# Gathers of v that wait for a free buffer of a ring of 40 instead of an earlier landing, with sixteen weighted rows and six banks for q

## What is computed

```python
for l in range(2):
    q = (x @ Wq[l] + bq[l]).reshape(N, H, D)       # k and v likewise
    a = (q[dst] * k[src]).sum(-1) * scale
    amax = segment_max(a, dst);  e = exp(a - amax[dst])
    denom = segment_sum(e, dst); alpha = e / (denom[dst] + 1e-16)
    agg = segment_sum(alpha[:, :, None] * v[src], dst)
    x = agg + (x @ Ws[l] + bs[l]) + enc
```

## Time and profile before

| what | us |
|---|---|
| median of three runs | 3386.14 (3384.03 to 3386.51) |
| the profiled execution, whole | 3403.18 |
| its span | 3401.4 |
| layer 0: first k gather issued, first v gather issued | 347.75, 774.83 |
| layer 0: last reduce of scores starts, first v product starts | 799.97, 841.80 |
| layer 0: last v gather issued, last v products start | 1265.48, 1269.47 |
| layer 1: first k gather issued, last v gather issued | 1532.71, 2455.14 |

### The profile page before, as it was taken

One profiled execution on the slowest core, in us unless ns is written; L12 is line 12 of the kernel. 1 busy time (PEld: TensorE's weight loads), 2 busy tenths in 40 slices (PEclk: granted clock), 3 DMA queues, 4 the chain that ended last, 5 costly groups with the idle time before them and its releaser, 6 DMA issues. The chain is left out here.

```text
span 3401.4 us, 43825 instructions
## 1 busy us (share of the span) xinstructions
PE 2660.2 (78%) x9872; PEld 1887.6 (55%) x9872; DVE 2266.3 (67%) x3504; ACT 829.6 (24%) x1638; POOL 1642.9 (48%) x1559
## 2 busy tenths in 40 slices
PE   2999787664877778997876658777776799969998
PEld 1788343333655556873443336555555577647776
DVE  5666688888766655446898887666547345476655
ACT  0454222221000011002222210000145323155544
POOL 0110667665566651106676656666514235344444
PEclk8999567776999998995667769999988899979999
DMA  1654666664566665436666646666642422261111
GB/s 58 211 197 171 196 195 198 193 191 124 161 194 198 198 184 180 139 115 200 193 199 194 193 116 173 192 194 193 183 168 99 136 99 99 85 198 38 37 37 36
DMA packets 215838, 524.38 MB, mean 154 GB/s; under 512 B 30652, under 2 KB 48424, under 8 KB 215238
## 3 DMA queue, kind: packets, MB, share of 16 engines
q0 software_dynamic: 100160, 328.28, 34.0%
q1 hardware_dynamic: 98182, 161.91, 14.2%
q10 hardware_dynamic: 17280, 31.63, 2.5%
HBM read 439.83 MB, written 81.88 MB: 153 GB/s over the span
## 5 line engine op out<-in xcount | busy, mean ns | idle before, releaser
L1488 PE MATMUL edge_psA<-layer_q_space 128*128 128x256 f32 (+1 forms) x2656 | 670.2, 400 | 200.0 <-DVE layer_q_space L1374 185.8
L1251 POOL DMA_INDIRECT edge_ring<-v_rows,edges_src x626 | 615.1, 983 | 370.6 <-DMA edge_ring<-v_rows,edges_src 197.3
L1251 POOL DMA_INDIRECT edge_ring<-k_rows,edges_src x626 | 591.5, 945 | 322.4 <-DMA edge_ring<-k_rows,edges_src 173.7
L1443 PE MATMUL edge_psQ<-layer_q_space,edge_hotT 128*128 x1328 | 575.3, 582 | 170.0 <-DVE layer_y_space L1296 132.6
L1488 PEld LDWEIGHTS edge_psA<-layer_q_space 128*128 128x128 f32 x2656 | 489.3, 193 | 380.7 <-issue 318.2
L1374 DVE TENSOR_TENSOR layer_q_space<-edge_ring,edge_psQ 128x512 f32<-128x512 f32 x664 | 434.6, 683 | 171.2 <-SPq L1219 168.0
L1443 PEld LDWEIGHTS edge_psQ<-layer_q_space,edge_hotT 128*128 128x128 f32 x1328 | 337.9, 279 | 373.2 <-issue 317.9
L1296 DVE TENSOR_TENSOR layer_y_space<-edge_psQ,edge_ring 128x512 f32<-128x512 f32 x664 | 423.7, 682 | 138.1 <-issue 52.1
L106 PE MATMUL proj_psP<-proj_w,proj_xT 128*128 128x512 f32 x1920 | 470.8, 403 | 12.6 <-DVE proj_w L886 5.5
L106 PEld LDWEIGHTS proj_psP<-proj_w,proj_xT 128*128 128x128 f32 x1920 | 361.8, 191 | 99.5 <-DVE proj_w L886 6.9
L1280 DVE TENSOR_REDUCE layer_scores<-layer_y_space 128x32 f32<-128x2048 f32 x166 | 377.6, 2275 | 0.1
(11 more groups left out here) (290 smaller groups left out, 2835.7 us busy)
## 6 DMA issues: line engine op xcount, KB each, us to landing
agg_rows<-layer_q_space ACTq DMA_DIRECT2D x40, 260.0 KB, 3.7
base_rows<-proj_enc SPq DMA_DIRECT2D x40, 256.0 KB, 2.0
k_rows<-proj_out ACTq DMA_DIRECT2D x40, 256.0 KB, 2.9
v_rows<-proj_out ACTq DMA_DIRECT2D x40, 256.0 KB, 2.5
edge_ring<-k_rows,edges_src POOLq DMA_INDIRECT x626, 3.7
edge_ring<-v_rows,edges_src POOLq DMA_INDIRECT x626, 3.7
ffn_downT<-down_rows SPq DMA_DIRECT2D x11, 512.0 KB, 10.2
proj_agg<-agg_rows SPq DMA_DIRECT2D x20, 260.0 KB, 3.0
```

The costliest lines, as they stand in the source:

```text
L1251: pool.indirect_dma_start(ring[:, (n + 1) % NB, :], None, rows, bass.IndirectOffsetOnAxis(ap=T["src"][:, t:t + 1], axis=0)).then_inc(lande ...
L1443: last = pe.matmul(psQ[i][:], hotT[j % 2][:, i * P:(i + 1) * P], one(qp[:, k, bass.ds(tiles[i], 1), :]), start=(k == 1), stop=(k == 0))
L1488: last = pe.matmul(psA[:, bass.ds(d % 2, 1), e, 0:hi - lo].rearrange("p o w -> p (o w)"), hot[:, s % R, :], wv[:, s % R, lo:hi], start=Fal ...
```

## The change

Five things change, all in `edge_attention` and the table that it reads.

1. The ring has NV = 40 buffers. k uses the first 32, and `prod` lies in the last eight during the k part. v uses all 40.
2. Gathers of k keep the wait for the landing three before. Gathers of v wait for no landing: the first 32 wait on `multiplied` as before, the next eight wait until all scores are reduced (`prod` is free), and gather t from 40 on waits until `weighted` has counted t - 40 + 21.
3. `wv` and `hot` have R = 16 rows instead of 8, so DVE starts a group at s when PE has summed slots up to s - 13.
4. q has six banks instead of four: two of `psA`, unused in the k part, are added.
5. PE waits for `hots` and `beside` once a group of 4 instead of in each slot. The arrival tables begin at other values (`K_FIRST`, `V_FIRST`) so that v starts at buffer 0.

```diff
-V_FIRST = ET % NB + 1
+NV = 40
+K_FIRST = NB - ET % NB
+V_FIRST = NV
...
-        B, R = 4, 8
+        B, R, QB = 4, 16, 6
...
-        ring = m.sb("ring", [P, NB, C])
+        ring = m.sb("ring", [P, NV, C])
...
-        prod = y_space[:, 0:2 * B * C].rearrange("p (i c) -> p i c", c=C)
-        cut = 2 * B * C
+        prod = ring[:, NB:NB + 2 * B, :]
+        cut = 0
...
+        psQ = [m.ps(f"psQ{i}", [P, C]) for i in range(B)] + [psA[:, 0, i, :] for i in range(QB - B)]
...
+        buffer = [(n + K_FIRST) % NB for n in range(ET)] + [t % NV for t in range(ET)]
+        landing = [(landed[u], 16 * buffer[:n + 1].count(u)) for n, u in enumerate(buffer)]
...
-                    if n >= FLIGHT:
-
-                        old = n - FLIGHT
-                        pool.wait_ge(landed[(old + 1) % NB],
-                                     old // NB * 16 + 16 if (old + 1) % NB else (old + 1) // NB * 16)
+                    if FLIGHT <= n < ET:
+
+                        pool.wait_ge(*landing[n - FLIGHT])
...
                     if t < NB:
                         pool.wait_ge(multiplied, min(n - NB + NT + 1, USED))
+                    elif t < NV:
+
+                        pool.wait_ge(reduced, BATCHES)
                     else:
-                        pool.wait_ge(weighted, t - NB + NT + 1)
+                        pool.wait_ge(weighted, t - NV + NT + 1)
...
-                        if j:
-
-                            pe.wait_ge(multiplied, j * B + i - B + 1)
+                        if j * B + i >= QB:
+
+                            pe.wait_ge(multiplied, j * B + i - QB + 1)
...
-                    pe.wait_ge(hots, s // B + 1)
-                    pe.wait_ge(beside, s // B + 1)
+                    if s % B == 0:
+                        pe.wait_ge(hots, s // B + 1)
+                        pe.wait_ge(beside, s // B + 1)
```

## The result

The changed kernel takes **3268.0 us** (median of 4 runs, 3264.0 to 3270.2) against 3385.1 us before (4 runs, 3381.2 to 3386.5), a ratio of 0.965 with a 95% interval of 0.964 to 0.967. It is faster by 117 us. The forecast was 3250 in a range of 3225 to 3292. The profiled execution takes 3264 us where that of before took 3403, so between the two traces there are 139 us.

A forecast was written before the change was run, and what follows sets the result against it. POOL's gathers, held by landing waits, were taken to bound the v part, and the k part was tied to POOL too. Layers gain 69.6 and 71.5 us, less 2 each: 137; 3386 - 137 = 3249, say 3250 us, range 3225 to 3292.

The forecast's parts named there:

- What bounds the v part: v part: runs at POOL's gather pace, 1.445 us each; 56 us a layer are waits beyond the floor, mostly under landings.
- The pace of 1.25 us: v part without the landing wait: POOL issues a gather every 1.25 us, its floor, and PE and DVE stay faster.
- Rival (a): v part: the DMA engines, or one, cap the pace above 1.25 us; at 1.35 the time is 3303; chance 0.13.
- (c): Slower: with only buffers limiting flight, landings lengthen and the stream slows; at 1.60 us a gather, 3440; chance 0.03.
- (d): v part: landings did not hold POOL, gaps stay; eight gathers and earlier start give 29 us, 3357; chance 0.02.
- Rival (b): k part: PE's banks made POOL's landings bunch, so k gains 10 us a layer instead of 2: 3233; chance 0.12.
- The eight more buffers and the start: v part: 273 gathers left instead of 281, at 1.25 us 64.6 and 66.5 us less; POOL resumes 3 us earlier.
- less 2 each: End of each layer: 2 us set against the gain, since a late landing there finds no slack in flight.
- The cover: Between the parts: the eight extra gathers cost nothing, done near 840, or 843 if blocked, long before they are needed.
- The banks of q: k part: six banks bounded per layer by 6 us won and 3 lost; 2 us won taken.
- The wait of DVE for PE in steady flow: v part: with sixteen rows the 25.4 us that L1364 waits for PE vanish, but buy nothing by themselves.
- The median: Last step: before's median lies 17 us below its profiled execution, carried over: 3386 - 137 = 3249, say 3250.

## Why the prediction was right, and where it was off

**What bounds the v part: right.** POOL's gathers, held by landings beyond 3.75 us. Taking out the landing wait alone (103 us) and keeping it alone (36 us of gain left) showed it from both sides, and a wait for the landing five before, which cost next to nothing, showed that it is the depth.

**The pace of 1.25 us: right to the digit.** 272 steps in 340.0 us in both layers. PE and DVE stayed below it. Rival (a), a cap by the DMA engines, is refuted up to this pace: their share rose to 0.76, forecast 0.77, and the stream to the 224 GB/s forecast. Rivals (c) and (d) are refuted as well: the median landing stayed at 3.7 us with no limit on the flight but the buffers, and the gaps went. Rival (b), 10 us a layer from the k part by the banks, is refuted too: with eight rows and four banks the way to the first v product was only 4.3 and 1.7 us longer.

**The eight more buffers and the start: right.** 64.6 + 3 and 66.5 + 3 us, less 2 each, were forecast for the v part. From DVE's first v product to the end of its last there were 429.0 and 431.1 us before and 362.3 and 362.4 after, so 66.7 and 68.7 less against 65.6 and 67.5. The pace made up some 54 a layer of it, the eight gathers and the earlier start the rest. The block that the Trainium skill names (SBUF — State Buffer, section Terms) showed under the second mask step, where the trace of before had no gather: a gather that began 1.1 us after the step took 2.75 us and ended 0.8 us after it. Under the six subtractions after it it did not show: the gathers there took 1.02 and 0.95. The cover held either way.

**The banks of q: right in size, hard to see.** I took 2 us a layer. From the first k gather to the first v product the change was -1.3 and -4.3 us in the first pair of traces, and +3.2 and -1.3 with the changed kernel's first later trace. Differences of 3 us between sessions hide a gain of 2. Within one session four banks and eight rows cost 4.3 and 1.7 us there, and 0.4 and 1.5 with free k gathers.

**The wait of DVE for PE in steady flow: read wrongly.** I expected the 25.4 us ahead of L1364 to vanish. After the change 18.6 us are still put down to PE there, and before and after it DVE's register instructions reach up to the end of nearly every such gap. Since the sum counts nothing for it, the forecast is not touched.

**The median: 18 us too low, and the step that failed is the last one.** The sum of 137 us against the profiled execution of before gave 3266; the profiled execution after took 3264. I then carried over the difference of 17 us between the profiled execution of before and its median. That difference is no property of a profiled execution: in three other sessions the kernel before runs at 3402 to 3405, profiled or not, and in two of them the changed one at 3275. The timed runs of before were faster by 17 us beside the result, those of the changed kernel by only 7. So of the 137, 127 came where both ran at their usual level, and 117 in the session of the result.

**The 2 us between 3266 and 3264 are partly luck.** Against the trace of before, the first trace of the changed kernel is 135.4 us shorter in the v parts and 5.6 from the first k gathers to the first v products, and 1.5 longer in all the rest. Its later trace on another chip is 134.3 shorter in the v parts, where 133 were forecast, but 1.9 longer in the k parts, where 4 less were forecast, and 3.5 longer in the rest, which the change doesn't touch. By these two traces that is 8 of the 10 us that the 127 lack to the 137. The changed kernel's profiled execution there is 10.5 us longer than the first one, mainly in the gathers of k (429.4 and 427.8 us in place of 425.0 and 424.3 from the first to the last), which still wait for landings.

Why before ran at 3385 in one session of four stays open. Landings shorter there would explain it, since they price both kernels and before the most, but the trace beside it took 3403 us, like those of the later sessions, so it can't show what made the timed runs faster.

**What I did not see: the k part.** I wrote that the landing wait stays there and priced everything else. I read it as tied to POOL, at 1.365 us a gather, and the same arithmetic would have given 313 x (1.365 - 1.25) = 36 us a layer. With the k gathers free, the way from the first of them to the first v product was 39.5 and 37.7 us shorter than in the changed kernel of the session.

## What to carry to other kernels

A wait for the landing of the n-th transfer before sets a pace: n issues must cover the late landings, not the median one. Here three in flight covered 3.75 us of a landing of 3.7 at the median and 6 at worst in the v part, and cost 0.19 us on each of 562 gathers; five cost next to nothing. Read the gaps of the issuing engine against its gap where nothing is waited for, and apply the finding to every stream of the kernel that has the same wait. And a forecast that rests on one profiled execution should give the change as a difference, with the level of the session as an uncertainty of its own.

## What was unexpected of the hardware

A gather that POOL was issuing when DVE scanned or took a mask step ended only after that DVE instruction (6.44, 3.46 and 2.75 us in place of 0.94), while float32 subtractions with both inputs in SBUF beside it cost at most 0.08 us (1.02 against 0.94). And the longest landings of every k part looked at, 8.2 to 10.1 us, are those of gathers issued beside the one transfer of 2016.5 KB; no other gather of k took longer than 5.8 us there. With three in flight they stopped POOL for 4.81 us in layer 0 of the kernel before, and without a landing wait not at all. No run leaves this transfer out, so that it is the cause is read from the times alone.
